# A mixer's output projection, its weights and inputs split into float32r parts in four slots of each group

## What is computed

```
x = x + mixer(layernorm(x))        # a state space mixer, the part that is changed
x = x + experts(layernorm(x))
x = x + attention(layernorm(x))
x = x + experts(layernorm(x))
```

```
gate, hBC, dt = split(x @ in_proj)
hs, B, C = silu(conv4(hBC));  dt = softplus(dt + bias)
Y_diag = (C B^T * decay) (hs * dt)          # inside a chunk
state  = state * decay + B^T (hs * dt * decay)
Y_off  = C state * decay                    # from earlier chunks
y   = (Y_diag + Y_off + hs * D) * silu(gate)
y   = y * rsqrt(mean over a group's 1024 channels of y^2 + eps) * norm_w
out = y @ out_proj                          # summed over the 8 groups
```

## Time and profile before

| | us |
|---|---|
| median of 3 runs | 2749.71 (2749.38 to 2751.24) |
| the profiled execution | 2748.32 |
| its span, first to last instruction | 2746.5 |
| TensorE busy | 2537.2 (92%) |
| VectorE busy | 1924.8 (70%) |
| ScalarE busy | 1452.7 (53%) |
| GpSimd busy | 392.4 (14%) |

### The profile page before, as it was taken

One profiled execution on the slowest core, in us unless ns is written; L12 is line 12 of the kernel. 1 busy time (PEld: TensorE's weight loads), 2 busy tenths in 40 slices (PEclk: granted clock), 3 DMA queues, 4 the chain that ended last, 5 costly groups with the idle time before them and its releaser, 6 DMA issues. The chain is left out here.

```text
span 2746.5 us, 42314 instructions
## 1 busy us (share of the span) xinstructions
PE 2537.2 (92%) x14144; PEld 1770.3 (64%) x14144; DVE 1924.8 (70%) x3759; ACT 1452.7 (53%) x3497; POOL 392.4 (14%) x448
## 2 busy tenths in 40 slices
PE   3579999999999999999999999996989889999799
PEld 2467777777776777776777677764874534444488
DVE  5367878777787787787877887865556467676354
ACT  2265656556657566566666565643223346666311
POOL 2101111111111111110110110122220011111121
PEclk7799999999999999999999999998999989999899
DMA  2322232223223223223323223212013111110000
GB/s 91 97 59 65 66 90 67 62 69 89 64 61 97 63 68 90 59 71 88 67 65 88 67 64 84 68 26 88 0 74 124 66 47 41 36 40 25 1 12 19
DMA packets 195003, 172.68 MB, mean 63 GB/s; under 512 B 31264, under 2 KB 157296, under 8 KB 193136
## 3 DMA queue, kind: packets, MB, share of 16 engines
q1 hardware_dynamic: 189344, 168.13, 22.3%
q10 hardware_dynamic: 5456, 2.00, 0.3%
HBM read 151.70 MB, written 18.38 MB: 62 GB/s over the span
## 5 line engine op out<-in xcount | busy, mean ns | idle before, releaser
L487 PE MATMUL bank<-xh,wh 128*128 128x512 f32 x1152 | 467.4, 406 | 49.4 <-DVE wl L838 33.6
L694 ACT ACTIVATE xch<-bank,pk 128x64 f32<-128x64 f32 x1024 | 219.9, 360 | 530.0 <-PE bank L569 528.9
L617 PE MATMUL bank<-wo,yt 128*128 128x512 f32 x1024 | 452.1, 594 | 16.7 <-issue 13.8
L487 PE MATMUL bank<-xl,wh 128*128 128x512 f32 x1152 | 452.3, 393 | 0.0
L487 PE MATMUL bank<-xh,wl 128*128 128x512 f32 x1152 | 452.2, 393 | 0.0
L812 DVE SCALAR_TENSOR_TENSOR cacc<-raw,cwh,cacc 128x512 f32<-128x512 f32 x480 | 360.5, 751 | 44.4 <-ACT cacc L796 32.9
L617 PEld LDWEIGHTS bank<-wo,yt 128*128 128x128 f32 x1024 | 192.9, 190 | 238.1 <-issue 235.3
L487 PEld LDWEIGHTS bank<-xh,wh 128*128 128x128 f32 x1152 | 218.4, 190 | 97.6 <-DVE wl L838 34.4
L487 PEld LDWEIGHTS bank<-xh,wl 128*128 128x128 f32 x1152 | 218.1, 189 | 47.7
L487 PEld LDWEIGHTS bank<-xl,wh 128*128 128x128 f32 x1152 | 218.7, 190 | 40.3
L2043 ACT ACTIVATE at_PT<-bank 128x512 f32<-128x512 f32 (+3 forms) x384 | 167.4, 498 | 118.3 <-PE bank L1958 113.8
(11 more groups left out here) (246 smaller groups left out, 4637.6 us busy)
## 6 DMA issues: line engine op xcount, KB each, us to landing
xn<-w_hs_dram SPq DMA_DIRECT2D x112, 256.0 KB, 2.7
EC<-ecum_scratch SPq DMA_DIRECT2D x112, 256.0 KB, 8.6
xn<-w_gate_dram SPq DMA_DIRECT2D x80, 256.0 KB, 3.0
wo<-w_out_dram SPq DMA_DIRECT2D x8, 2048.0 KB, 9.1
rawx<-w_gate_dram SPq DMA_DIRECT2D x48, 256.0 KB, 3.1
rawx<-w_hs_dram SPq DMA_DIRECT2D x48, 256.0 KB, 2.7
qk_scratch<-at_part SPq DMA_DIRECT2D x48, 256.0 KB
at_qT<-qk_scratch SPq DMA_DIRECT2D x32, 192.0 KB, 2.6
```

The lines of the kernel that those rows point to most:

```text
L487: mm = nc.tensor.matmul(BA[bank][:, :], w[:, s, k, :], x[:, k, tok], start=(k == 0 and m == 0), stop=(k == KC - 1 and m == 2))
L617: mm = nc.tensor.matmul(BA[b][:, :], yt[:, j * P:(j + 1) * P], wo[:, j, :], start=(j == 0), stop=(j == JT - 1))
L694: o = nc.scalar.activation(xch[:, hh * HP:(hh + 1) * HP], BT[1 - u][:, i * HP:(i + 1) * HP], ACT.Copy, scale=pk[:, h, c, O_DT + hh:O_DT + ...
```

## The change

The output projection's channel tiles are split in the way of the input projections: yt into yh and yl, wo into woh and wol (the low parts lie in the memory of the originals). A split channel tile takes three float32r products, the others one in float32. `SPLIT = (0, 2, 4, 4, 6, 8, 8, 8)` says how many of the eight are split in each slot: two tiles of weights are split in each of the slots 1, 2, 4 and 5 (`ac_out_high`, `dv_out_low`), and stay so until the group's end. To make place for the split copies,

- the residual stream is kept in DRAM: 128 tokens are loaded into one of two buffers xz, summed and stored back in each slot, and the first expert layer begins with loading all of x;
- the squares are written over the chunk's own columns in act2, not to a buffer of their own.

The order changes too. ScalarE makes yh and the squares right behind the first gate tile's tanh; the copies of convolution tiles move ahead of clamps and weighing. TensorE makes the second half of the decay differences after the first convolution tile, and in slots 3 and 7 the second half of the transposes after the output projection.

```diff
...
+        xr = sb(top, "xr", [P, NT, C])
...
+        s_xr = [sem(top, f"d_residual{i}") for i in range(2)]
...
+                sp.dma_start(xr[:, 0, :], x_dram[0:P, :]).then_inc(s_xr[0], 16)
+                sp.dma_start(xr[:, 1:, :], x_dram[P:, :].rearrange("(z p) c -> p z c", p=P)).then_inc(s_xr[1], 16)
...
+        def shared(name, shape):
+
+            with nc.sbuf_tensor(name, shape, F32) as whole:
+                pass
+            return whole, sb(ctx, name + "_lo", shape, F32R)
...
-        wo = sb(ctx, "wo", [P, JT, C])
+        wo, wol = shared("wo", [P, JT, C])
+        woh = sb(ctx, "woh", [P, JT, C], F32R)
...
-        sq = sb(ctx, "sq", [P, JT, P])
...
-        yt = sb(ctx, "yt", [P, GC])
+        yt, yl = shared("yt", [P, GC])
+        yh = sb(ctx, "yh", [P, GC], F32R)
...
+        xz = sb(ctx, "xz", [P, 2, C])
...
+        SPLIT = (0, 2, 4, 4, 6, 8, 8, 8)
...
+        def squares(n):
+
+            h, c = n % NT // CH, n % CH
+            return act2[:, h, 0:JT, c * P:(c + 1) * P]
...
-            if not last and mine:
+            late = step and not mine
+            if not last and not late:
                 pe_hidden(pe, *nxt, 1)
...
-            if not last:
+            if not last and not mine:
                 pe_diff(pe, *nxt, (2, 3))
-                if not mine:
-                    pe_hidden(pe, *nxt, 1)
...
                 tile(r)
-            pe.wait_ge(wo_set, 17 * g + 17)
+                if r == 0 and not last:
+                    pe_diff(pe, *nxt, (2, 3))
...
             b = bank()
             dv_gg.wait(pe, n + 1)
-            for j in range(JT):
-                mm = nc.tensor.matmul(BA[b][:, :], yt[:, j * P:(j + 1) * P], wo[:, j, :], start=(j == 0), stop=(j == JT - 1))
+            pe.wait_ge(wo_set, 17 * g + 17)
+            terms = [(yt, wo, j) for j in range(SPLIT[z], JT)]
+            terms += [(y, w, j) for j in range(SPLIT[z]) for y, w in ((yh, woh), (yh, wol), (yl, woh))]
+            for i, (y, w, j) in enumerate(terms):
+                if i == JT - SPLIT[z]:
+                    dv_wo.wait(pe, 4 * g + SPLIT[z] // 2)
+                    dv_yl.wait(pe, 7 * g + z)
+                mm = nc.tensor.matmul(BA[b][:, :], y[:, j * P:(j + 1) * P], w[:, j, :],
+                                      start=(i == 0), stop=(i == len(terms) - 1))
             mm.then_inc(pe_out.sem, 1)
+            if late and not last:
+                pe_hidden(pe, *nxt, 1)
...
+        def newly_split(z):
+
+            return slice(SPLIT[z - 1], SPLIT[z]) if z and SPLIT[z] > SPLIT[z - 1] else None
+
+        def ac_out_high(act, g, z):
+
+            js = newly_split(z)
+            if js is not None:
+                act.wait_ge(wo_set, 17 * g + 17)
+                nc.scalar.copy(woh[:, js, :], wo[:, js, :]).then_inc(ac_wo.sem, 1)
...
+            late = step and not mine
+            ac_out_high(act, g, z)
             if not last:
                 ac_xdt(act, *nxt, 0)
-                if mine:
+                if not late:
                     ac_xdt(act, *nxt, 1)
             if step:
                 ac_gate_tanh(act, step, 2 * (z % CH), bank())
+            dv_gg.wait(act, n + 1)
+            if SPLIT[z]:
+                cols = slice(0, SPLIT[z] * P)
+                nc.scalar.copy(yh[:, cols], yt[:, cols]).then_inc(ac_yh.sem, 1)
+            nc.scalar.activation(squares(n), yt[:, :].rearrange("p (j t) -> p j t", j=JT), ACT.Square).then_inc(ac_sq.sem, 1)
...
-            dv_gg.wait(act, n + 1)
-            pe_ss.wait(act, n)
-            nc.scalar.activation(sq[:, :, :], yt[:, :].rearrange("p (j t) -> p j t", j=JT), ACT.Square).then_inc(ac_sq.sem, 1)
+            copy(0)
             if not last:
                 ac_relu(act, *nxt, 2)
                 ac_relu(act, *nxt, 3)
             weigh(0)
-            copy(0)
             weigh(1)
+            copy(1)
+            tanh(0)
             if not last:
                 ac_exp(act, *nxt, 2)
                 ac_exp(act, *nxt, 3)
-                if not mine:
+                if late:
                     ac_xdt(act, *nxt, 1)
-            copy(1)
-            tanh(0)
             weigh(2)
             weigh(3)
             copy(2)
...
+                    pe_ss.wait(dve, 8 * p[0] - 4)
...
+                    pe_ss.wait(dve, 8 * p[0])
...
+            sq = squares(n)
...
+        def dv_y_low(dve, g, z):
+
+            if SPLIT[z]:
+                cols = slice(0, SPLIT[z] * P)
+                ac_yh.wait(dve, 7 * g + z)
+                ac_sq.wait(dve, 8 * g + z + 1)
+                nc.vector.tensor_tensor(yl[:, cols], yt[:, cols], yh[:, cols], ALU.subtract).then_inc(dv_yl.sem, 1)
+
+        def dv_out_low(dve, g, z):
+
+            js = newly_split(z)
+            if js is not None:
+                ac_wo.wait(dve, 4 * g + js.stop // 2)
+                pe_out.wait(dve, 8 * g + z)
+                nc.vector.tensor_tensor(wol[:, js, :], wo[:, js, :], woh[:, js, :], ALU.subtract).then_inc(dv_wo.sem, 1)
...
+            dv_y_low(dve, g, z)
             for p, i in left:
                 dv_silu_tile(dve, p, i)
             if step:
                 dv_gate_tile(dve, step, 2 * (z % CH) + 1, bank(), n + 1)
+            dv_out_low(dve, g, z)
...
-            nc.vector.scalar_tensor_tensor(xr[:, z, :], BA[b][:, :], rr[:, 1:2], xr[:, z, :], ALU.mult, ALU.add)\
+            dve.wait_ge(d_xin[n % 2], 16 * (n // 2 + 1))
+            nc.vector.scalar_tensor_tensor(xz[:, n % 2, :], BA[b][:, :], rr[:, 1:2], xz[:, n % 2, :], ALU.mult, ALU.add)\
                 .then_inc(dv_out.sem, 1)
...
+                def load_x(n):
+
+                    if n >= 8 * G:
+                        return
+                    if n >= 2:
+                        sp.wait_ge(d_xout[n % 2], 16 * (n // 2))
+                    src = A["x"] if n < NT else x_dram
+                    sp.dma_start(xz[:, n % 2, :], src[n % NT * P:(n % NT + 1) * P, :]).then_inc(d_xin[n % 2], 16)
+
+                def store_x(n):
+                    dv_out.wait(sp, n + 1)
+                    sp.dma_start(x_dram[n % NT * P:(n % NT + 1) * P, :], xz[:, n % 2, :]).then_inc(d_xout[n % 2], 16)
+
+                load_x(0)
+                load_x(1)
...
+                    if z > 0:
+                        store_x(8 * g + z - 1)
...
+                    if 0 < z:
+                        load_x(8 * g + z + 1)
...
+                    store_x(8 * g + 7)
+                    load_x(8 * g + 9)
                 for z in range(NT):
                     slot_loads(G - 1, z, True)
+                store_x(8 * G - 1)
+                for i in range(2):
+                    sp.wait_ge(d_xout[i], 16 * 4 * G)
...
+                    if isinstance(z, int) and z < 2:
+                        dve.wait_ge(s_xr[z], 16)
...
```

More of the change, by code:

```diff
@@ L108, in build @@
         turned = sem(top, "turned")
-        mixer(nc, A, xr, ident, identb, nhalf, stat, mv, rstd, xn, BANK, pack_dram, rows_dram, ecum_dram, skip_dram, sb, sig, sem, turned, debug)
+        mixer(nc, A, x_dram, ident, identb, nhalf, stat, mv, rstd, xn, BANK, pack_dram, rows_dram, ecum_dram, skip_dram, sb, sig, sem, turned, debug)
+        xr = sb(top, "xr", [P, NT, C])
         wgu = sb(top, "wgu", [P, KC, 2, F])
@@ L145, in _, with mixer @@
                 sp.wait_ge(s, 16)
-def mixer(nc, A, xr, ident, identb, nhalf, stat, mv, rstd, xn, BANK, pack_dram, rows_dram, ecum_dram, skip_dram, sb, sig, sem, turned, debug):
+def mixer(nc, A, x_dram, ident, identb, nhalf, stat, mv, rstd, xn, BANK, pack_dram, rows_dram, ecum_dram, skip_dram, sb, sig, sem, turned, debug):
     with ExitStack() as ctx:
@@ L442, in mixer @@
         d_rw, d_ec = sem(ctx, "d_rw"), sem(ctx, "d_ec")
+        d_xin = [sem(ctx, f"d_xin{i}") for i in range(2)]
+        d_xout = [sem(ctx, f"d_xout{i}") for i in range(2)]
         RAW, TAP = 3, TAPS - 1
         BA, BT, BD, BY = BANK[0:2], BANK[2:4], BANK[4:6], BANK[6:8]
+        SPLIT = (0, 2, 4, 4, 6, 8, 8, 8)
         headed = lambda ap: ap.rearrange("p (h c) -> p h c", c=HP)
@@ L1165, in prologue @@
                         ac_exp(act, 0, 0, q)
-                run(act, ac_slot, prologue, (ac_hi, ac_tail, ac_raw, ac_th, ac_xc, ac_mn, ac_ex, ac_tg, ac_sq))
+                run(act, ac_slot, prologue, (ac_hi, ac_tail, ac_raw, ac_th, ac_xc, ac_mn, ac_ex, ac_tg, ac_yh, ac_sq, ac_wo))
             @block.vector
@@ L1185, in prologue @@
                     dv_masked(dve, 0, 0, range(NQ))
-                run(dve, dv_slot, prologue, (dv_lo, dv_cv, dv_act, dv_sm, dv_M, dv_yo, dv_yd, dv_sg, dv_gg, dv_st, dv_out, dv_r, dv_sq))
-    if debug is not None:
-        debug_dump(nc, debug, "x1", xr, sem)
+                run(dve, dv_slot, prologue, (dv_lo, dv_cv, dv_act, dv_sm, dv_M, dv_yo, dv_yd, dv_sg, dv_gg, dv_yl, dv_wo, dv_st, dv_out, dv_r, dv_sq))
 def norm_transpose(eng, kind, S, xr, ident, nhalf, stat, mv, rstd, xn, xnT, banks):
@@ L1279, in ffn @@
         s_rev = SG["rev"]
```

(2 more changed lines are left out.)

17 lines of the change are left out of this document (9 added, 8 removed).

## The result

The changed kernel takes 2830.24 us, the median of 4 runs (2828.60 to 2833.83), 1.0292 times the time before (95% interval 1.0279 to 1.0305). That is 80 us slower: the side that was forecast, but beyond the 2797 us and beyond the range's upper end of 2822. The profiled execution has a span of 2827.7 us, 81.2 more than before.

The account below looks back on a forecast made before the run. TensorE, busy 1577 of 1595 us, was taken to bound the kernel. Terms -57.5 + 43 + 22.7 + 12 + 13 + 8 + 6 = +47, added to 2748.3 plus 1.4, gave 2797 us, range 2747 to 2822.

Parts of the forecast that it names:

- products: Output projection on TensorE: three float32r products replace one float32, saving 0.18 us per split channel tile, 57.5 us in all.
- waits at squares and slot 4's tile: Slots 1, 2, 4, 5, 6: TensorE waits for VectorE's folds and a low weight part, +43 us.
- slot 7 into slot 0: Seven group changes: late differences, transposes and scaling delay GpSimd's decay product, residual and copies; 3.25 us each, +22.7 us.
- slot 0's order on ScalarE: Slot 0, eight times: ScalarE idles before convolution tile 0's copy, now ahead of clamps and weighing; 1.5 us each, +12 us.
- last four slots, waits: Without gate tiles as cover, scaling, cast and square ahead of the clamps make TensorE wait: +13 us (8 to 16).
- mixer's end: Residual's store and reload, 2 MB, go ahead of the expert weights that ScalarE waits for: +8 us (5 to 10).
- clock: New waits in slot 0 and three of the last slots: four of eleven lose 1.6 us to 1.2 GHz, +6 us.
- The rival on the clock: The clock falls after each of the eleven new waits: 2808 us; chance 0.12.
- Exclusion: VectorE instructions with two SBUF inputs wait for GpSimd's decay product, giving the larger waits at the squares, within the +43 us.
- the first rival: No exclusion: VectorE and GpSimd run side by side and the clock holds, +43 becomes 9: 2757 us; chance 0.23.
- ScalarE's order: Slot 0: tile 0's copy ahead of clamps and weighing leaves ScalarE idle 2.2 us, the projection waiting near 3 us.
- The chain at slot 7: Slot 7 into slot 0: scaling, GpSimd's decay product, power, residual and copies all move 2.66 us, delaying TensorE's transposes; +22.7 us.

Follow-up runs that it names:

- Experiment 1: Changed kernel with products nobody reads filling TensorE's waits before slot 0's projection, behind slot 7's sum of squares and before slot 5's: 2803.46 us.
- Experiment 13: Kernel of experiment 10 with no channel tile split, so every tile in float32: 2757.81 us, ratio 1.0026 to the kernel before.
- experiment 8: Changed kernel with GpSimd's decay product waiting for VectorE's folds in slots 1, 2, 4, 5 and 6: 2793.73 us.
- experiment 6: Changed kernel with SPLIT all zero, so no casts and low parts of y and of the output weights: 2816.27 us.
- experiment 7: Changed kernel with VectorE's two subtractions moved behind the first convolution tile in slots with convolution tiles: 2800.07 us.
- experiments 3 to 5: 3: changed kernel, late transposes put back, residual's store and reload later in SyncE's queue, 2806.14 us; 5: changed kernel, only decay differences back behind the state, 2826.05 us.
- experiment 4: Third experiment's kernel with the earlier order restored: clamps and first weighing ahead of ScalarE's first copy, TensorE's decay differences behind the state: 2779.48 us.
- experiment 11: Kernel of experiment 10 with the projection's products reordered, those needing the newest weights' low part last, each kind with its own wait: 2728.98 us.
- experiment 10: Changed kernel with experiments 4 and 7, last four slots' further splits dropped and ScalarE reordered there, expert weights loaded ahead of most of the residual: 2749.70 us.

## Why the prediction was right in kind and wrong in size

The sum's terms, and what the two traces and the runs give for each:

| term of the sum | predicted us | measured us | from |
|---|---|---|---|
| products | -57.5 | -53.5 | TensorE's starts, 6.69 per group at full clock |
| waits at squares and slot 4's tile | +43 | +34.8 | 28.0 + 6.8 |
| slot 7 into slot 0 | +22.7 | +18.5 | 6.8 (L541) + 10.8 (L516) + 1.0 (L529) |
| slot 0's order on ScalarE | +12 | +9.5 | 7.2 (L645) + 2.3 (a tile), groups 1 to 7 |
| last four slots, waits | +13 | +12.9 | 9.48 (L541) + 4.66 (L645) - 1.21 (L607) |
| mixer's end | +8 | +9.4 | last projection to the end |
| clock | +6 | up to 37 | 78.2 us at half the clock, 3.4 before: the difference, halved |

Six terms are within 9 us of the trace, and together they came out at 31.6 us, where the sum had 41.2. **The step that failed is the last one:** "The new waits in slot 0 (3.0 us) and in three of the last slots are of the first size, eleven in all; I count four such losses of 1.6". It took 2.87 us as the size of a wait that brings the clock down, because 1.72 had not the earlier trace rows, and then counted four of its eleven places without giving a reason. After, the clock came down behind all seven waits of 2.7 us in slot 0 from group 1 on (not behind the same wait in group 0) and four times in the last four slots. It also came down behind 1.54 us at slot 0's start in 5 of 7 groups, and behind 1.40 to 2.02 us in slot 5 in 4 of 7, waits that the prediction had itself computed (1.8 and 1.45) and left at full clock. Experiment 1 shows the size: 27 us for the 16 stretches ahead of the last four slots, with nothing changed but the filling. The 37 is an upper bound for all 20. With 37 for 6 the sum would have been near 2828, and that with some luck: the other six terms were 9.6 too high, and 12.6 us were in no term. The rival on the clock (2808) had its mechanism right, and stayed low because it counted only eleven places.

The seven terms sum to 68.6 of the 81.2 us, with the clock at its upper bound. Of the rest, 2.4 are in the first slot, and about 8 in slots 1, 2 and 5, where the sum of squares and the tile behind it start 0.1 and 0.2 us later though no wait is recorded. Experiment 13 has these 8 us too, without any split; their cause is open, as are the 2 us or more then left.

**Exclusion** was right: experiment 8 shows it by itself, and the first rival falls. The trace of before had more for it than the prediction's one mask: 37 masks of 1.2 us, each ending 0.55 us behind GpSimd's product. After, low parts as long as 2.06 us stand there. The Trainium skill says (SBUF — State Buffer, Who interferes with whom) that a VectorE instruction with two SBUF inputs contends with a GpSimd instruction that reads SBUF, and that the shared ports are an exclusive lock. Both traces agree: subtractions are held up in the changed kernel (2.06 instead of 0.68 us), taps in experiment 8 (2.28 instead of 0.75). But the waits at the squares need the subtractions' own time too: without casts and subtractions (experiment 6), or with the subtractions alone moved (experiment 7), low parts stay long and the squares do not wait. Either repair removes most of the 28 us, so they can't be shared out between the two.

**ScalarE's order** was right, as rows and experiments 3 to 5 show: 2.12 us idle, 2.75 of waiting, and the wait back at 1.64 in experiment 4. **The chain at slot 7** was right in its start and near in its size (18.5 for 22.7), but TensorE met it earlier than forecast. It waited 1.54 us at the product for B, which needs the scaling itself (it ends at 1079.39 + 1.74 = 1081.13, the product starts at 1081.24). Of the wait forecast for the copies of B and C, behind GpSimd's power and the residual, 0.49 us in two of seven groups was left. What the prediction missed is how the two cover each other: undoing the chain gave 6 us of the 19 expected, since the queue was next. "The SP queue waits at a group's end for the store, but what is behind it is needed much later: 0" was true of the changed kernel only, whose slot 0 ran late anyway; once it did not, that queue cost 18 us.

**The split** itself: 0.167 us per channel tile against 0.18 forecast. That three products cost less than one was never the question; in the changed kernel's order splitting lost 14 us, in the mended one it won 29 (experiment 11 against 13).

## What to carry to other kernels

Where one engine sets the pace, price each new wait on it twice: its length, and what its clock loses behind it; count every wait as long as those seen here to do so (1.4 us and more) as one that may, not only those as long as the first one seen. Before adding work to an engine with room on average, look at which neighbour runs beside the exact place, and whether the two can run together. When a repair gives less than its wait, look for the next instruction that had been waiting behind it, on the DMA queue too, before dropping the theory.

## What the runs showed of the hardware

- What a stretch at 1.2 GHz cost depends on what stood there. 3.4 us of it made slot 0's projection 1.7 us longer (8.83 against 7.13), and slot 5 1.6 us longer than in the groups without one; at slot 0's start it cost 1.1 (groups without it wait 0.49 us there for the copies of B and C).
- A wait's length alone does not tell whether low clock follows: the same 1.45 us in slot 7 had none in the changed kernel and in experiment 1 (7 groups each), in experiment 4 one in two groups, in experiment 10 in every group, in experiment 11 in three. What else counts was not tried.
- The residual's stores of 256 KB took 2.0 to 11.4 us to land (8.6 in the median of 64), the output's stores of the same size 2.0; the residual's reloads took 3.0 and the loads of EC, also 256 KB, 8.4. So size alone does not give the time, and a queue that waits for such a store stands for as long.
- A VectorE instruction that GpSimd's decay product held up ended 0.55 us behind that product, in all 37 such rows of each of three traces (before, the changed kernel, experiment 8), and the row shows it as one long instruction, not as a wait.
